# A graph network layer pair on one Trainium2 core: seven of 762 indirect gathers replaced by single-row copies from SyncE

## What is computed

```python
def layer0(z, edge_weight, src, dst, Wm, bm, W1, b1, W2, b2):
    msgs = z[dst] @ Wd + z[src] @ Ws + edge_weight[:, None] * ww[None, :] + bm
    agg = segment_max(msgs, dst)             # 0 where a node has no edge
    hidden = relu(z @ W1a + agg @ W1b + b1)
    return hidden @ W2 + b2
def sage_conv(x, src, dst, Wl, bl, Wr):
    mean = segment_sum(x[src], dst) / maximum(degree, 1)
    return mean @ Wl.T + bl + x @ Wr.T
x = layernorm(x + layer0(x, ...))
x = layernorm(x + sage_conv(relu(sage_conv(x, ...)), ...))
```

## Time and profile before

| what | value |
|---|---|
| runs of the kernel before | 1210.14, 1210.36, 1215.10 us; median 1210.36 us |
| profiled execution | 1212.98 us, its span 1211.2 us |
| mean granted clock of TensorE | 0.824 |
| PE busy | 1091.0 us, 90% of the span |
| DVE busy | 854.4 us, 71% |
| POOL busy | 753.2 us, 62% |
| ACT busy | 368.4 us, 30% |
| DMA, mean over the span | 95 GB/s |

### The profile page before, as it was taken

How to read it: one execution, slowest core, us unless ns; L and a number is a source line. 1 busy time by engine, 2 the same in 40 slices (tenths; PEclk the granted TensorE clock), 3 DMA queues, 4 the chain that set the end, 5 groups by cost and what they waited for, 6 DMA issues and landing times. The chain is left out here.

```text
span 1211.2 us, 23176 instructions
## 1 busy us (share of the span) xinstructions
PE 1091.0 (90%) x6892; PEld 803.7 (66%) x6927; DVE 854.4 (71%) x3105; ACT 368.4 (30%) x1189; POOL 753.2 (62%) x789
## 2 busy tenths in 40 slices
PE   5798998998989888898999898988989988989998
PEld 5467776776777766776767667666766666555554
DVE  6487767777777678768786787787777876365444
ACT  3242333332333333333333332333333333131000
POOL 4777777777777777777777777777777771000000
PEclk9797767777678688758885797887788989999999
DMA  7332333333333333333433344333444333352110
GB/s 189 103 98 78 91 90 88 90 105 88 89 90 102 93 101 92 89 103 102 104 89 84 96 118 114 86 95 90 108 113 114 91 95 112 96 160 59 31 31 24
DMA packets 114462, 114.76 MB, mean 95 GB/s; under 512 B 23267, under 2 KB 99514, under 8 KB 114330
## 3 DMA queue, kind: packets, MB, share of 16 engines
q1 hardware_dynamic: 87244, 60.68, 18.3%
q0 software_dynamic: 25024, 51.30, 16.4%
q10 hardware_dynamic: 2061, 1.20, 0.4%
HBM read 100.42 MB, written 12.68 MB: 93 GB/s over the span
## 5 line engine op out<-in xcount | busy, mean ns | idle before, releaser
L798 POOL DMA_INDIRECT area<-zs_d,area x762 | 729.9, 958 | 232.3 <-issue 229.6
L968 DVE TENSOR_TENSOR_SCAN area<-area,bank 128x512 f32<-128x512 bf16 x196 | 248.8, 1270 | 231.0 <-PE bank L1302 220.9
L667 ACT CAST adj_w<-bank 128x325 f32 x391 | 176.0, 450 | 623.4 <-PE bank L1362 594.6
L1356 PEld LDWEIGHTS bank<-area 128*128 128x128 f32 x1564 | 263.4, 238 | 39.1 <-ACT area L675 15.3
L1356 PE MATMUL bank<-area 128*128 128x13 f32 x1564 | 269.1, 285 | 15.7 <-issue 10.1
L949 DVE TENSOR_SCALAR area<-area 128x325 bf16<-128x325 f16 x782 | 252.0, 322 | 0.0
L948 DVE TENSOR_SCALAR area<-area 128x128 bf16<-128x128 f16 x782 | 211.5, 270 | 0.3 <-PE bank L1362 0.3
L1359 PE MATMUL bank<-area 128*128 128x325 bf16 x782 | 208.3, 355 | 0.0
L1302 PE MATMUL bank<-ident,area 128*128 128x128 f32 x762 | 151.7, 332 | 62.6 <-DMA area<-zs_d,area 62.3
L1302 PEld LDWEIGHTS bank<-ident,area 128*128 128x128 f32 x762 | 96.7, 163 | 120.6 <-DMA area<-zs_d,area 81.6
L1343 PE MATMUL bank<-ident,area 128*128 128x128 f32 x782 | 157.3, 336 | 0.2 <-issue 0.2
(11 more groups left out here) (159 smaller groups left out, 846.3 us busy)
## 6 DMA issues: line engine op xcount, KB each, us to landing
area<-mask_d SPq DMA_DIRECT2D x195, 128.0 KB
area<-zs_d,area POOLq DMA_INDIRECT x762
area<-wp_d SPq DMA_DIRECT2D x585, 3.0 KB
area<-parts_d SPq DMA_DIRECT2D x16, 384.0 KB, 7.5
zr_d<-area SPq DMA_DIRECT2D x24, 128.0 KB
area<-zr_d SPq DMA_DIRECT2D x6, 512.0 KB, 3.9
parts_d<-area SPq DMA_DIRECT2D x23, 96.0 KB
adj_w<-in_x_dram SPq DMA_DIRECT2D x3, 512.0 KB, 5.9
```

Of the source, the lines that this page charges most:

```text
L667: nc.scalar.copy(adj[:, :, bass.ds(at, W)], A_BANK[s % 2][:, 0:COLS].rearrange("p (h w) -> p h w", w=W))
L798: pool.indirect_dma_start(gring[:, g % GR * 4 + s % 2 * 2 + u, :], None, x if g < RAW else zs_d[0:N, :], bass.IndirectOffsetOnAxis(ap=src_ ...
L968: nc.vector.tensor_tensor_scan(S[:, g % 2, 0:n], mask[:, g % MR, 0:n], T_BANK[g % 2][:, 0:n], S[:, (g + 1) % 2, 511:512] if g else 0.0, AL ...
L1356: nc.tensor.matmul(o[:, 384:384 + W], St[:, b * P:(b + 1) * P], sel[:, g % 2, u, s % 2, :], start=u == 0, stop=u == 1)
```

## The change

For seven groups, g = 32, 58, 84, 110, 136, 162 and 188 (`OWN`, every 26th), GpSimd leaves out the fourth gather. SyncE copies those 128 rows of zs_d one by one, each with a DMA of 512 B whose source row is in a register. It does so over the 26 slots before the group, five rows in a slot, behind load_edges(k) and ahead of everything else of that slot. The row numbers come from src by a small DMA two slots before, and are read into registers 16 at a time, at the slots 0, 3, 6, 9, 12, 16, 19 and 22 of the 26. The rows go to one of two buffers (`own`, the free half of raw_l), with a semaphore each; PE waits for it before the fourth transpose of such a group. The count of landed gathers that PE waits for is 3 instead of 4 in these groups. SP waits for the stores of zs before its loop.

```diff
+ROWS = 5
+STEP = -(-P // ROWS)
+OWN = tuple(range(STEP + 6, NG - 2, STEP))
+def landings(g):
+    return sum(4 - (i in OWN) for i in range(g % GR, g + 1, GR))
...
+                nodes = []
+
+                def own_rows(k):
+                    for i, g in enumerate(OWN):
+                        at = (4 * g + 3) * P
+                        if k == g - STEP - 2:
+                            if i >= 2:
+                                sp.wait_ge(t_ps, OWN[i - 2] + 1)
+                            sp.dma_start(own_r[:, i % 2, 0:P], src[at:at + P].rearrange("(o e) -> o e", o=1)).then_inc(l_own_r, 16)
+                        for r in range(max(0, (k - g + STEP) * ROWS), min(P, (k - g + STEP + 1) * ROWS)):
+                            if r == 0:
+                                sp.wait_ge(l_own_r, 16 * (i + 1))
+                            if r % RC == 0:
+                                nodes[:] = nc.values_load_multi_w_load_instructions(
+                                    own_r[:, i % 2, r:r + RC], engines=[mybir.EngineType.SP], min_val=0, max_val=N - 1,
+                                    skip_runtime_bounds_check_because=NODES)[1]
+                            sp.dma_start(own[r:r + 1, i % 2, :], zs_d[bass.ds(nodes[r % RC], 1), :]).then_inc(l_own[i % 2], 16)
+
                 sp.wait_ge(wp_st, 16 * (BB - 1))
+                sp.wait_ge(zs_st, 16 * NX)
                 for k in range(NG + 5):
                     if 2 <= k < NG:
                         load_edges(k)
+                    own_rows(k)
...
                 for s in supers(g):
-                    for u in range(2):
+                    for u in range(1 if g in OWN and s % 2 else 2):
                         pool.indirect_dma_start(gring[:, g % GR * 4 + s % 2 * 2 + u, :], None, x if g < RAW else zs_d[0:N, :],
...
-                    pe.wait_ge(landed[g % GR], 64 * (g // GR) + 16 * (n // P))
+                    pe.wait_ge(landed[g % GR], 16 * (landings(g) - 4 + n // P))
                     for b in range(n // P):
-                        last = nc.tensor.matmul(o[:, b * P:(b + 1) * P], gring[:, g % GR * 4 + b, :], ident[:, :],
+                        rows = gring[:, g % GR * 4 + b, :]
+                        if g in OWN and b == 3:
+                            i = OWN.index(g)
+                            pe.wait_ge(l_own[i % 2], 16 * P * (i // 2 + 1))
+                            rows = own[:, i % 2, :]
+                        last = nc.tensor.matmul(o[:, b * P:(b + 1) * P], rows, ident[:, :],
                                                 start=False, stop=b == n // P - 1, is_transpose=True)
```

More of the change, by code:

```diff
@@ L36 @@
 LATE = NT - 3
+ROWS = 5
+STEP = -(-P // ROWS)
+OWN = tuple(range(STEP + 6, NG - 2, STEP))
 ORDER = (5, 0, 1, 2, 3, 4, 6)
+NODES = "a source node, which is below N"
 STARTS = "a superbatch's first destination node, which is below N"
@@ L174, in gnn_kernel @@
             (f16, COLS + 1), (bf16, NT + 1), (bf16, W + 1), (bf16, 4, 3 * F), (f32, 2, 512))
+        own = raw_l[:, 1, 2 * F:4 * F].rearrange("p (a f) -> p a f", f=F)
         ws = quad.rearrange("p a b -> p (a b)").bitcast(f32)[:, 0:F]
@@ L181, in gnn_kernel @@
         d0_r = edge[64:65].bitcast(i32).rearrange("p a b -> p (a b)")
+        own_r = edge[96:97].bitcast(i32)
         (_, x1_0, gres, b2b, _, w1l, w2_0, gparts, late, w2_1, sc_0, zrT, hB, sc_1, x1_1) = carve(
@@ L234, in gnn_kernel @@
         raw_ps, raw_sb = sem("raw_ps"), sem("raw_sb")
+        l_own_r, l_own = sem("l_own_r"), [sem(f"l_own{i}") for i in range(2)]
         landed = [sem(f"landed{i}") for i in range(GR)]
@@ L1281, in raw_T @@
             def raw_T(g):
-                pe.wait_ge(landed[g % GR], 64 * (g // GR) + 64)
+                pe.wait_ge(landed[g % GR], 16 * landings(g))
                 pe.wait_ge(x_sb, NX)
```

## The result

| | before | after |
|---|---|---|
| median of the runs | 1212.73 us (1210.14 to 1222.74, 4 runs) | 1285.39 us (1283.75 to 1295.96, 4 runs) |
| profiled execution, span | 1212.98, 1211.2 | 1285.34, 1283.5 |
| mean granted clock | 0.824 | 0.817 |

The change makes the kernel slower: 1.059 times the time of before, 95% interval [1.0545, 1.0642]. The forecast was 1218 us in a range of 1201 to 1245. The sign was right, the size and the range were wrong.

A forecast was written before the change was run, and what follows sets the result against it. POOL's gathers were taken to bound the kernel until about 1000 us, then PE. PE: 7.6 us early, 13.5 lost, 2.26 and 2.71 regained, so 0.9 late; plus 6.6 of clock, 7.5 slower: 1218 us, range 1201 to 1245.

The forecast's parts named there:

- what the sum said: On GpSimd (POOL), leaving out seven gathers at 1.26 us each was to remove 8.8 us.
- On average it fits, with 12% left.: On SP, copies and register loads were to take 539 us of about 613 us of waiting for the scan.
- The mask and wp loads stand this.: On SP, load slots pass 1.8 to 2.5 us to the next slot; its mask and wp loads were to tolerate it.
- gather waits follow in which PE catches up.: At earlier quads (slots 49, 70, 105, 113, 137, 140), PE was to recover partial losses in later gather waits.
- The last four quads: Quads at slots 169, 172, 175 and 178, in PE's stretch without gather waits: together 13.5 us late.
- that are caught up: Quads of the earlier stretches, whose lateness PE was to make good in later gather waits; no loss in the sum.
- a carry of one slot: On SP, lateness that a slot loading registers passes to the next: about 1.8 to 2.5 us.
- SP becomes the bound: Rival, chance 0.10: at 0.45 us a copy, SP's work equals all its waiting; at 0.50 us the time is 1252.
- Three spells of 2.2 us: On PE, three late-quad waits each put 5 us of work at the low clock: 6.6 us in all.

The follow-up runs named there:

- the kernel of 0.993: The changed kernel with one DMA of 128 fixed rows replacing each group's row copies, and no register loads left in the program: 1205.38 us against 1210.65 before, ratio 0.9931.

## Why the prediction was wrong

**Right: what bounded the kernel, and nearly the prices.** POOL's 1.26 us a gather held, and seven of them are worth what the sum said: 0.7% with SP left alone. A copy takes 0.42 us against 0.37, inside the range that was given for it; a load of 16 registers takes 3.52 us, 3.6 with its gap, against 3.66; a bare slot 3.43 us against 3.2. SP's wait for the scan was to fall to about 100 us and fell to 116.4. I also asked whether a load of 16 values would cost no more than one of a few; the trace refuted that: it took 3.52 us. The medians here are 0.92, 1.32 and 3.52 us for 3, 5 and 16 values, which is 0.2 us a value and 0.33 us beside it. The Trainium skill, "Runtime: NRT & Kernel Launch", section "Instruction fetch mechanics", gives some 200 ns for each register; it speaks of loads from HBM, and these loads from SBUF agree.

**Wrong: "On average it fits, with 12% left."** With the measured prices SP was given 896 x 0.42 + 56 x 3.6 + 2 = 580 us instead of 539, of 613: 5% left, or 3% by the slot (4.83 of 5.0 us). So the average did fit, barely, and fitting on average was taken for fitting. It leaves out that SP can't work ahead: the mask of slot g waits for the scan of group g - 2, so what a bare slot leaves over is lost unless SP is behind at that time. A load slot has 7.0 to 7.5 us of issues in 5.0 and puts SP over 2 us behind; a bare slot gives back 5.0 - 3.43 = 1.6, or less where a store or a tile stands in it, and the next load slot comes in three. Where such things stand between, the lumps overlap, and SP is behind most of the time: it waits in 53 slots where it waited in 191.

**Wrong: "The mask and wp loads stand this."** This was read from one pair of slots, 171 and 172, with a carry of one load slot. With the carries of several, wp_d loads land late 33 times, 60.1 us; the sum had 0 there. It is the second largest term.

**Wrong: "gather waits follow in which PE catches up."** This step let me price four quads out of fifteen. The gather waits are there in the trace of before, but they are 62.3 us for the whole program, and I never set the lateness of all the quads and wp loads against that number. The quads alone take 74.8, so the gather waits are used up (0.0 is left of them) and what goes beyond them reaches the end. The last four quads, priced at 13.5 us, measured 4.31 + 6.59 + 4.53 + 6.48 = 21.9, and the eleven "that are caught up" 52.9.

**Too small in the same step: what a quad loses.** It was priced as the copies, a carry of one slot and 3.74 us of landing. The landing was right (3.6 to 4.4 us), the carry wasn't: at slot 49 the copies of the slot before ran until 287.72, and PE's wait was 7.53 us where this reckoning gives 1.85 + 1.8 = 3.65. The largest waits were to be at slots 70, 113 and 178; they are at 81 (8.4), 145 (7.9) and 49, and slot 70 has 2.9.

**The loop that closes it.** SP's slot starts when the scan of two groups back is done, the scan follows PE, and PE now follows SP's quads and wp loads. Lateness that once was absorbed by POOL's pace (PE waiting for gathers) now holds POOL, through the ring: 96.7 us. That this closes a loop is read from the waits; no run cuts it open. It is the case "SP becomes the bound", given 0.10, with the wrong point of decision: it was put at copies of 0.45 us, where the sum equals all of SP's waiting. With the copies at 0.42 us it had already come.

**The clock.** Three spells of 2.2 us were put in for stretches at the lower level after a wait. Nothing of the kind shows: PE's busy time is 1092.7 us against 1091.0, so the waits do not come back as slower matmuls in the total. This term was 6.6 of the 7.5 us of the forecast, and without it the forecast was 0.9 us, no change. That the sign came out right is luck. The windows show where it is lower and where higher (busy, instructions, granted clock, DMA share, GB/s), first after, then before:

```profile
54.00:103.00 49.00, 49.00 (x206) 0.50 0.26 69
103.00:500.00 397.00, 334.78 (x2194) 0.77 0.35 89
...
900.00:1040.00 140.00, 106.84 (x697) 0.80 0.33 88
```

```profile
54.00:103.00 49.00, 44.06 (x323) 0.93 0.35 90
103.00:500.00 397.00, 358.20 (x2239) 0.73 0.35 92
...
900.00:1040.00 140.00, 126.78 (x893) 0.93 0.35 96
```

From 54 to 103 us the changed kernel runs at the 1.2 GHz level throughout and does 206 matmuls where 323 were done. That doesn't make the loss: the kernel with three copies a slot has the same stretch, and the time of before:

```profile
54.00:103.00 49.00, 49.00 (x208) 0.50 0.31 72
```

Nor does every kernel with copies have it: the one with copies and no loads does 334 matmuls there, at a granted clock of 0.92.

**What stays open.** Of the 34 us by which the span with the copies last is longer than before (1245.5 - 1211.2), PE is busier for 18.4 (1109.4 - 1091.0); the rest is idle time, in which waits for wp_d (45.4) and parts_d (31.8) have taken the place of those for gathers. Why PE is busier there and with five registers a slot (1128.2), and not in the change itself, wasn't settled; the kernel of 0.993 has 1101.2, so part of it comes without any loss. No kernel had late wp loads with early quads alone. How full SP may be was not closed in either, beyond the pairs of the table. And that SP can't work ahead was not tried: the masks and wp loads have two buffers each, and no kernel gave them a third.

## What to carry to other kernels

Before work is given to an idle engine, set it against the worst run of slots and not against the sum of its waits: an engine whose slot starts at an event of the others can't bank what it leaves over. Here, with 349 of 644 us of its waiting left, no loss showed; with 116 left it was 6%. The waits of the engine that feeds the end, for the resource being relieved, are what the program can absorb in lateness; add up every new wait against that one number. What has to be given anyway goes behind the loads with the nearest due time, which here gave back 42 of 73 us.

## What was not expected of the hardware

A register load on SP costs mostly by the value: medians of 0.92 us for 3, 1.32 for 5, 3.52 for 16, and 0.46 us for the single value that the kernel before loads at its start. Splitting loads to smooth them therefore adds about 0.33 us for each piece, an estimate from these medians; 42 of the 182 loads of the run with five registers a slot took only some 0.8 us for their five, and why is open. A row copy with its address in a register costs SP more than one with a fixed address, 0.42 against 0.30 us from one to the next, though the DMA instruction itself is no longer (0.228 against 0.252): the two address steps of 0.037 and 0.029 us and the gaps around them make the difference. Register loads that nothing uses are not in the program that runs, so a kernel that is to show their price has to use them. And a chip can be 290 us slower for every version of a kernel, with pauses of several engines together, and there hide the gain of the seven gathers (0.9977 and 1.0 where 0.993 was measured elsewhere) while it keeps the loss where SP is full (1.061).
